# A graph-network kernel: 25 instead of 24 ranges of edges scattered, and 768 instead of 800 gathers in the messages, with the first edges of visits found by plain transfers

## The reference

```python
h = relu(layernorm(x))
x = x + gcn(relu(gcn(h)))            # two graph convolutions, as below
h = relu(layernorm(x))
msg = relu(concat(h[src], edge_attr) @ W1 + b1)
agg = segment_sum(msg, dst) / max(count(dst), 1)
x = x + relu(concat(h, agg) @ W2 + b2)

def gcn(x):                          # deg counts the edges of a target, and itself
    h = x @ W;  norm = dinv[src] * dinv[dst];  dinv = deg ** -0.5
    return segment_sum(h[src] * norm, dst) + (self loop) + b
```

## Time and profile before

| | |
|---|---|
| median of 3 runs | 2456.9 us (2456.45 to 2467.43) |
| the profiled execution | 2462.0 us, its span 2460.1 us |
| PE busy | 2155.0 us (88%) |
| DVE busy | 1870.1 us (76%) |
| POOL busy | 1822.6 us (74%), 1,687 instructions |
| ACT busy | 1241.6 us (50%) |

### The profile page before, as it was taken

One profiled execution on the slowest core, in us unless ns is written; L12 is line 12 of the kernel. 1 busy time (PEld: TensorE's weight loads), 2 busy tenths in 40 slices (PEclk: granted clock), 3 DMA queues, 4 the chain that ended last, 5 costly groups with the idle time before them and its releaser, 6 DMA issues.

```text
span 2460.1 us, 45677 instructions
## 1 busy us (share of the span) xinstructions
PE 2155.0 (88%) x15568; PEld 1771.9 (72%) x15569; DVE 1870.1 (76%) x3574; ACT 1241.6 (50%) x3349; POOL 1822.6 (74%) x1687
## 2 busy tenths in 40 slices
PE   0344899999999998799995599999999999999996
PEld 0133679997667897688884487887787878888885
DVE  6999999998889884544447377777777777777777
ACT  5846246665666773555557243444444434444440
POOL 0867877888888787777777777777777777777770
PEclk9867999999999998999998799999999999999999
DMA  9414233333334351588874243434434343434432
GB/s 359 173 39 140 74 127 127 135 126 126 124 124 163 141 188 45 166 325 302 322 282 149 70 145 103 142 109 121 131 106 145 106 141 109 131 120 118 133 86 60
DMA packets 127247, 358.89 MB, mean 146 GB/s; under 512 B 34082, under 2 KB 77831, under 8 KB 117687
## 3 DMA queue, kind: packets, MB, share of 16 engines
q10 hardware_dynamic: 24752, 186.56, 19.9%
q0 software_dynamic: 56880, 85.25, 13.5%
q1 hardware_dynamic: 45369, 84.00, 9.9%
HBM read 229.75 MB, written 125.93 MB: 145 GB/s over the span
## 4 chain that ended last, share of the span: by engine, by line
PE 52%; POOL 17%; DVE 15%; issue 8%; ACT 4%; DMA 3%; DVEq 1%; POOLq 0%; ACTq 0%; SPq 0%
POOL rows L803 14%; PE ps_feat L1102 6%; PE ps_node L1102 6%; PE ps_node L1117 5%; PE ps_feat L1117 5%; DVE region_c L2079 5%; PE ps_sum L1212 3%; ACT rows L1318 3%; PE pre_banks L1090 3%; PE ps_extra L1250 3%; POOL permuted L821 2%; PE pre_banks L1203 2%; PE ps_feat L1234 2%; PE ps_node L1234 2%; PE ps_sum L1234 2%
## 5 line engine op out<-in xcount | busy, mean ns | idle before, releaser
L821 POOL DMA_INDIRECT permuted<-rows_or_lows,slot_of_edge x768 | 902.5, 1175 | 234.0 <-issue 151.7
L803 POOL DMA_INDIRECT rows<-table,region_a x800 | 786.1, 983 | 243.8 <-issue 236.8
L2079 DVE TENSOR_TENSOR region_c<-iota_key,region_c 128x1568 bf16<-128x1568 f16 (+1 forms) x327 | 355.8, 1088 | 0.0
L1435 ACT ACTIVATE region_a<-pre_banks 128x392 bf16<-128x392 f32 x392 | 195.0, 499 | 146.3 <-PE pre_banks L1090 138.3
L1102 PE MATMUL ps_node<-region_a,region_b 128*128 128x256 bf16 (+1 forms) x1911 | 263.8, 268 | 4.1 <-issue 4.1
L1102 PE MATMUL ps_feat<-region_a,region_b 128*128 128x256 bf16 x1764 | 252.5, 272 | 0.0
L584 DVE CAST wide_counts<-region_a 128x1024 fp32r<-128x1024 bf16 (+2 forms) x163 | 117.2, 723 | 156.4 <-PE ps_node L1117 69.1
L1250 PE MATMUL ps_extra<-msg_parts,target_hot 128*128 128x256 f32 x1176 | 222.7, 305 | 13.8 <-DVE msg_parts L2264 13.6
L582 ACT ACTIVATE wide_counts<-region_a 128x1024 fp32r<-128x1024 bf16 x150 | 158.6, 1060 | 120.7 <-PE ps_node L1117 56.9
L2279 DVE TENSOR_TENSOR target_hot<-consts,region_a 128x512 fp32r<-128x512 f32 x336 | 207.5, 618 | 1.0
L1212 PE MATMUL ps_sum<-onehot,rows 128*128 128x64 f32 x1600 | 202.3, 270 | 0.0
(11 more groups left out here) (319 smaller groups left out, 4790.0 us busy)
## 6 DMA issues: line engine op xcount, KB each, us to landing
counts<-region_a ACTq DMA_DIRECT2D x23, 3136.0 KB
region_a<-counts ACTq DMA_DIRECT2D x11, 3200.0 KB
region_a<-counts ACTq DMA_DIRECT2D x11, 3072.0 KB
rows_or_lows<-block_lows ACTq DMA_DIRECT2D x72, 448.0 KB
permuted<-region_b SPq DMA_DIRECT2D x25, 833.0 KB, 24.4
region_a<-permuted SPq DMA_DIRECT2D x24, 833.0 KB
rows_or_lows<-edge_cols_in POOLq DMA_DIRECT2D x24, 544.0 KB
region_a<-attr_t_in SPq DMA_DIRECT2D x50, 256.0 KB, 2.8
```

The source lines that it names most:

```text
L803: nc.gpsimd.indirect_dma_start(rows[:, s, j * D:(j + 1) * D], None, tables[2], bass.IndirectOffsetOnAxis(ap=message_rows[:, c * TC + j:c * ...
L821: nc.gpsimd.indirect_dma_start(permuted, bass.IndirectOffsetOnAxis(ap=slot_of_edge[:, r * RT + k:r * RT + k + 1], axis=0), edge_rows_of[:, ...
L1435: nc.scalar.activation(counts[strip % 2][:, :, j * W:j * W + W], count_banks[w % BANKS][:, 0:KEYS].rearrange("p (d h) -> p h d", h=SB), AC ...
L2079: v.tensor_tensor(hot_key(u)[:, :, 0:n], iota_key[:, None, 0:n].to_broadcast([P, UNIT // SIDE, n, SIDE]), keys[:, :, None, :].to_broadcast ...
```

## The change

- RANGES 24 to 25: 32 more scatters (800), 14 more units (350), 8 fewer chunks (192) and 32 fewer gathers (768) in the messages; the loop has 352 steps. PACED becomes (17, 6): the range more stands beside the windows. Late ranking starts a strip earlier (LATE_STRIP 9). There is one blank store more into `permuted`.
- The first edges of the visits are no longer gathered by GpSimd. 19 plain transfers from DRAM to DRAM (`spread_starts`), ten from SyncE and nine from ScalarE, write each target's start as often as it has visits (2,688 words of 4 bytes); SyncE loads the result as a tile of 21 rows; VectorE shifts and converts it, TensorE turns it, VectorE adds the plan. VectorE does this ahead of the degrees of the nodes, before node phase 0, no longer in its middle.
- 14 scatters of range 0 (AHEAD_OF_VISITS) stand on GpSimd ahead of the gathers of the visits' edges.
- Ranges 2 to 13 are staged by SyncE; GpSimd stages 0 and 1 and those from 14 on.
- In `late_ranks` VectorE waits for its first operation right behind it, no longer before the second.

```diff
-RANGES = 24
+RANGES = 25
-LATE_STRIP = 10
+LATE_STRIP = 9
-PACED = (16, 6)
+PACED = (17, 6)
+STAGED_BY_SP = 14
+AHEAD_OF_VISITS = 14
...
+        def spread_starts(engine, run):
+
+            visit, target, n, k, step = run
+            of = starts_dram[target:target + n * step].rearrange("(n w) a -> n w a", w=step)[:, 0:1].to_broadcast([n, k, 1])
+            engine.dma_start(visit_starts_dram[visit:visit + n * k].rearrange("(n k) a -> n k a", k=k), of,
+                             allow_slow_non_contiguous=True).then_inc(starts_gathered, 16)
...
+            sp.wait_ge(starts_moved, 16)
+            for run in START_RUNS[0::2]:
+                spread_starts(sp, run)
+            sp.wait_ge(starts_gathered, 16 * len(START_RUNS))
+            sp.dma_start(visit_starts_i, visit_starts_dram.rearrange("(b p) a -> b (p a)", p=P)).then_inc(starts_gathered, 16)
...
+                    for r in range(2, STAGED_BY_SP):
+                        stage(sp, r)
...
-            pool.wait_ge(starts_moved, 16)
-            for b in range(VB):
-                nc.gpsimd.indirect_dma_start(
-                    visit_start[:, b:b + 1], None, starts_dram,
-                    bass.IndirectOffsetOnAxis(ap=visit_plan[:, 0, b:b + 1], axis=0)).then_inc(starts_gathered, 16)
-            pool.wait_ge(visit_rows_ready, 1)
+            pool.wait_ge(blanked, 16 * (RANGES + 1))
+            scatter(0, end=AHEAD_OF_VISITS)
+            pool.wait_ge(visit_rows_ready, 3)
...
             ranks_taken(EARLY - 1)
+            dve.wait_ge(starts_gathered, 16 * len(START_RUNS) + 16)
+            link(v.tensor_single_scalar(visit_starts_i, visit_starts_i, 4, ALU.arith_shift_right))
+            v.tensor_copy(visit_starts, visit_starts_i).then_inc(visit_rows_ready, 1)
             with dve.If(mixed < 1):
                 dve.wait_ge(starts_turned, 2)
                 v.tensor_copy(count[:, 0:SB], ps_sum[1][:, 0:SB])
                 dve.drain()
+            dve.wait_ge(visit_rows_ready, 2)
+            v.tensor_tensor(visit_row[:], ps_sum[0][:, 0:VB], visit_plan[:], ALU.add).then_inc(visit_rows_ready, 1)
```

More of the change, by code:

```diff
@@ L81 @@
 LATE_STEPS = (1, 2, 3, 6, 8)
-VISIT_ROWS_AT = 5
 SECOND_SPLIT_UNIT, SECOND_KEYS_UNIT = 4, 7
@@ L116, with runs_of @@
 BUILT_BEFORE = [max((v + 1 for v in range(u) if KEY_PARTS[v] & KEY_PARTS[u] or v % HOT_UNITS == u % HOT_UNITS), default=0) for u in range(UNITS)]
+VISIT_TARGETS = [(w * W + j * (W // len(splits)), k) for w, splits in zip(WINDOW_AT, SPLITS) for j, k in enumerate(splits)]
+def runs_of(parts):
+    runs, visit = [], 0
+    for target, k in parts:
+        if runs and runs[-1][3] == k and (runs[-1][2] == 1 or target - runs[-1][1] == runs[-1][2] * runs[-1][4]):
+            first, at, n, _, step = runs[-1]
+            runs[-1] = (first, at, n + 1, k, step if n > 1 else target - at)
+        else:
+            runs.append((visit, target, 1, k, W))
+        visit += k
+    return runs
 VB = (sum(VISITS) + P - 1) // P
+START_RUNS = runs_of(VISIT_TARGETS + [(0, VB * P - sum(VISITS))])
 VISIT_PARTS = [range(0, 13), range(13, VB)]
@@ L584, in widen, with staged, stage @@
                 nc.vector.tensor_copy(to, of).then_inc(widened["dve"], 1)
+        def spread_starts(engine, run):
[3 more added lines that the diff above has]
+                             allow_slow_non_contiguous=True).then_inc(starts_gathered, 16)
+        def staged(engine, r):
+            if 2 <= r < STAGED_BY_SP:
+                engine.wait_ge(rows_staged_by_sp[r % 2], 16 * (r // 2))
+            else:
+                engine.wait_ge(rows_staged[r % 2], 16 * (1 + max(r // 2 - (STAGED_BY_SP // 2 - 1), 0)))
+        def stage(engine, r):
+            if r >= 2:
+                engine.wait_ge(scattered[r % 2], (r // 2) * RT * 16)
+            engine.dma_start(edge_rows_of[:, r % 2], t["edge_cols"][:, r * RT:(r + 1) * RT].rearrange("p t c -> p (t c)")
+                             ).then_inc((rows_staged_by_sp if 2 <= r < STAGED_BY_SP else rows_staged)[r % 2], 16)
         @block.sync
@@ L806, in gather_messages, with scatter @@
                         ).then_inc(e["gathered"][s], 16)
-            def stage(r):
-                pool.dma_start(edge_rows_of[:, r % 2], t["edge_cols"][:, r * RT:(r + 1) * RT].rearrange("p t c -> p (t c)")
-                               ).then_inc(rows_staged[r % 2], 16)
-            def scatter(r, pace=lambda k: None):
+            def scatter(r, pace=lambda k: None, first=0, end=RT):
                 pool.wait_ge(ranked, r + 1)
-                pool.wait_ge(rows_staged[r % 2], 16 * (r // 2 + 1))
-                for k in range(RT):
-                    if k == RT // 2 and 1 <= r < RANGES - 1:
-                        pool.wait_ge(scattered[(r - 1) % 2], ((r - 1) // 2 + 1) * RT * 16)
-                        stage(r + 1)
+                staged(pool, r)
+                for k in range(first, end):
+                    if k == RT // 2 and STAGED_BY_SP <= r + 1 < RANGES:
+                        stage(pool, r + 1)
                     pace(k)
@@ L838, in beside_phase @@
                 pool.wait_ge(G["tab"], group(n, i * NG // (PHASED[n] * RT)) + 1)
-            stage(0)
-            stage(1)
+            stage(pool, 0)
+            stage(pool, 1)
             pool.wait_ge(loaded, 16 * N_LOADS)
@@ L876, in _ @@
                 for r in range(PHASED[n]):
-                    scatter(next(ranges), lambda k: beside_phase(n, r * RT + k))
+                    scatter(next(ranges), lambda k: beside_phase(n, r * RT + k), first=0 if n else AHEAD_OF_VISITS)
                 if n == 0:
@@ L1327, in _ @@
                                              accum_out=starts[:, 2, b:b + 1]).then_inc(searched, 1)
+            act.wait_ge(starts_moved, 16)
+            for run in START_RUNS[1::2]:
+                spread_starts(act, run)
             act.wait_ge(degree_ready, 1)
@@ L1969, in node_phase @@
                         rests(g)
-                        if n == 0 and g == VISIT_ROWS_AT:
-                            find_visits()
                 else:
```

46 lines of the change are left out of this document (20 added, 26 removed).

## The result

| | before | after |
|---|---|---|
| median of 4 runs | 2458.2 us | 2491.6 us (2489.0 to 2492.8) |
| ratio | | 1.0127, 95% interval 1.0105 to 1.0150 |
| profiled execution, span | 2462.0, 2460.1 us | 2491.6, 2489.8 us |
| visits' gathers start | 187.57 us | 193.22 us |
| first gather of the messages | 1371.09 us | 1403.51 us |

A forecast was written before the change was run, and what follows sets the result against it. GpSimd was taken to bound the kernel up to the messages, there GpSimd and TensorE a few per cent apart; -2 + 1 - 2 = -3 on 2462.0 gives 2459, less 5.1 over the median: 2454 us, range 2437 to 2472.

The forecast's parts named there:

- Part 1: Up to the messages' first gather: starts landed at 157 us, visits' gathers at 168 instead of 187.57; in all -2 us.
- the lower bound: Landing of the starts: 3 us of issues, 2.3 to 2.9 landing, 2.3 load, so 157 us at best.
- rival 2: Start: the transfers land late and move the first gather one for one; plausible 30 us gives 2469, bound 2499; chance 0.13.
- The rule that I quoted: Plain transfers: spread over the largest number up to 16 dividing the slowest dimension on both sides; counted as nothing.
- 786 scatters and 11 stagings: GpSimd behind the visits' gathers, from 202 us: 1.471 us a scatter and 0.9 us a staging.
- 1368.1: Forecast time in us of the messages' first gather, where it was 1371.1 before.
- VectorE's 25.8 us to spare: At the seam of scatters and gathers: VectorE's wait for rows, taken to cover 10 us of its added work.
- 19.6 us won at the start: Visits' gathers earlier by 19.6 us; with 10 from stagings, set against 26.5 for 18 more scatters.
- Part 2: The messages: GpSimd's gathers 41 us less, but TensorE's units set the pace; 1029.5 us, +1, perhaps 2 less at the end.
- rival 1: Messages: TensorE's stalls go with GpSimd's, faster, 2441 or even 2425 us; chance 0.27 beyond 0.5%.
- rival 3: Messages: TensorE waits on its ring with ScalarE and VectorE, 19 us of waits stay, slower, 2473 us; chance 0.08.
- The price of a unit: TensorE in the messages: 2.17 us a unit, beside 1.37 us a chunk, from a 335 us stretch without standing still.

The follow-up runs named there:

- run 1: The changed kernel with each plain transfer of 32 or more targets cut so that 16 divides the larger piece's count: 2474.9 us, ratio 1.0060.
- run 2: The changed kernel with the transfer of 452 targets cut into 449, a prime, and 3: 2519.0 us, ratio 1.0231.
- run 3: On top of run 1, the seven transfers of one target issued with the copies as outer dimension, in pieces that 16 divides and a rest: 2473.6 us.
- run 8: The kernel before with 12 stagings issued by SyncE instead of GpSimd and two semaphores of the late ranks merged: 2457.8 us, ratio 0.9989.
- run 4: The changed kernel with 24 ranges again (pace of 16, first late rank in strip 10), all else as changed: 2473.5 us, ratio 1.0056.
- run 5: The changed kernel with the whole first range, 32 scatters instead of 14, ahead of the visits: 2496.0 us, ratio 1.0147.
- run 9: The changed kernel (25 ranges) with even pieces, VectorE taking the starts in group 3 of node phase 0, without its stall: 2480.1 us, ratio 1.0089.
- run 6: On top of run 5, the second range's scatters no longer wait for windows of counts: 2534.1 us, ratio 1.0306.
- run 7: On top of run 6, a small VectorE write without input behind the one-hots of each of the first 80 units: 2487.4 us, ratio 1.0103.

## Why the prediction was wrong, step by step

**Failed: "Part 1", the landing.** I put it at 157 us, "I take the side of the lower bound, since the plain transfers overlap", and it was 191.9, inside my own bounds (up to 61 us of transfers; 40 measured). The visits' gathers came at 193.2 for 168: 25.2 us. No row stood behind the lower bound: the trace had no transfer of single words, and the time from one plain transfer's issue to its landing stood in for it. It is rival 2's mechanism, with 0.13 of the chance; its "plausible 30 us" was 40. The rule that I quoted and kept out of the sum named the cause: the same words in pieces that 16 divides took 24 us, with a prime count 70 (runs 1 and 2). As to the Trainium skill, "DMA: Bandwidth & Descriptors", section "Why a DMA increments its semaphore by 16 and not by 1": it takes the slowest dimension that is not of size 1, which fits run 3, and 24, 40 and 70 us for 233, 847 and 1,521 words on the fullest engine agree with its spread in order. They give no fixed price of a word.

**Mis-sized: 786 scatters and 11 stagings**, 1178.5 us for 1166.1, 12.4 more. Of that some 7 is the stagings: run 8 has them at 0.3 us each, not 0.9, so moving 11 of them won 3 us, not 10. The rest I only argue: a scatter costs what VectorE's work beside it lets it, and the average of the whole stage isn't the price of one more. By the rows of run 4 it is 1.58 us beside the windows (728.1 us for 460, 719.9 for 454 before) and 1.36 behind them (422.5 for 310), stagings included. The visits' gathers took 31.8 us for 34.0. So 1368.1 + 25.2 + 12.4 - 2.2 = 1403.5.

**Wrong in the reasoning, though the number held:** that a late landing moves the messages through GpSimd's chain. Runs 1 and 2 confirm one for one; run 5 shows that the way leads through VectorE's stall, the windows' start and the pace of the windows. The same miss added up that way: the windows 26.8 us late, and 8.6 of the extra range (below), make the 35.4 us between 1368.1 and 1403.5. Time that GpSimd wins ahead of the windows counts until range 0 is done, and what it wins beyond that is lost at the gate. Also wrong: VectorE's 25.8 us to spare; the whole table must be stored before the first gather, which leaves 14 (run 4). That a gather waits for nothing but buffers, as is said of the kernel before, holds only behind the first.

**The extra range.** From the windows' start, with 32 scatters done, to where the gathers could begin, 25 ranges take 1150.6 us and 24 take 1108.1 (252.6 to 1360.7): 42.5 us (run 4). I had most of that paid by 19.6 us won at the start. Run 9 has no stall and visits' gathers at 183.4, and costs 0.9%: the landing alone doesn't explain the result. Even had all 32 been done when the windows start at 226.1, the first gather would come at 226.1 + 1150.6 = 1376.7, 8.6 behind my 1368.1 and 5.6 behind the kernel before; this is worked out, the case wasn't run. Of the measured 32.4 us, then, 26.8 are the late windows and 5.6 the range.

**Right: "Part 2".** Forecast +1 and perhaps -2; measured 1026.3 against 1028.8. Rivals 1 and 3 fall. The price of a unit holds: 115 units and 63 chunks in the 335 us give 2.16 us where I had 2.17. GpSimd's 32 gathers fewer, with the 14 units that take their place, buy 2.5 us.

**Right as far as it was tested: 14 scatters ahead are free for GpSimd** (137.0 to 161.2 us). They do count: with 32 scatters begun before the windows start the first gather comes 1150.6 us behind that start, with 22 (run 9) 1162.4 us. What goes beyond 32 has no buyer (run 5). That the 14 slow no transfer beside them wasn't tested, and 32 did (run 5). That SyncE's stagings hold nothing up: right too; the last went out at 819.5 us for 746.

## What to carry to other kernels

Before a change spends one engine's time to relieve another, ask what the relief is worth after the next gate: here 32 gathers fewer gave 2.5 us, and 32 scatters more took 42. A wait's length is not the slack of the engine that waits; look for what else of its work others wait for. And a transfer of single words has no bandwidth to reason with: choose outer counts that 16 divides, and put no engine's only queue behind its landing.

## What the runs showed of the hardware

- 2,688 words of 4 bytes from DRAM to DRAM took 40 us, from the first issue to that of the load behind the last landing, as 19 plain transfers; 24 us as 24 with outer counts that 16 divides; 70 us with one of 449. In the first, one issue on each queue took 12.6 and 21.8 us of the engine's own time, in the last one took 38.3; with even pieces none took more than 1.4. That an unevenly spread transfer under way is what held them is argued.
- With 32 instead of 14 scatters beside them the same 19 transfers took 45 to 48 us (runs 5 to 7).
- An indirect transfer issued by GpSimd took 56.86 us instead of 0.95, beside a gapless stream of TENSOR_TENSORs on VectorE, in a kernel whose runs all lay within 2532.0 to 2534.9 us. With one small instruction without an input (0.06 us) in each pair no scatter took more than 3.1 us.
- Near the start of the windows GpSimd's scatters come each 1.485 us, as VectorE's pairs of one-hots do, instead of each 1.26 as at the end of the scatters (1401 to 1403.5 us).
